# Contiguous query tiles for the row maxima, and the softmax shift turned by TensorE instead of by a DMA

## The reference, cut to what matters

```
q = (xn @ Wq.T + bq) * 16**-0.5;  k = xn @ Wk.T + bk;  v = xn @ Wv.T + bv   # per head: 2048 x 16
scores = einsum('bqhd,bkhd->bhqk', q, k)
probs  = softmax(scores, axis=-1)
out    = einsum('bhqk,bkhd->bqhd', probs, v) @ Wo.T + bo
x + out + ffn(xn)
```

## Time and profile before

| what | value |
|---|---|
| median of 3 runs | 3491.28 us (3490.54 to 3492.51) |
| the profiled execution, its own time | 3490.54 us |
| its span, first to last instruction | 3488.5 us |
| TensorE busy | 3355.6 us, 96% |
| VectorE busy | 2889.4 us, 83% |
| ScalarE busy | 2453.4 us, 70% |
| TensorE weight loads busy | 1892.9 us, 54% |
| mean granted TensorE clock | 0.977 |

### The profile page before, as it was taken

The page is one execution under the profiler, slowest core; times in us unless marked ns, Lnnn a source line. Parts: engine busy times, 40 slices in busy tenths (PEclk is TensorE's granted clock), DMA queues, the critical chain, the costliest instruction groups (busy, mean ns, idle before and its releaser), DMA issues. The chain is left out here.

```text
span 3488.5 us, 69413 instructions
## 1 busy us (share of the span) xinstructions
PE 3355.6 (96%) x19824; PEld 1892.9 (54%) x19824; DVE 2889.4 (83%) x2923; ACT 2453.4 (70%) x4702; POOL 927.9 (27%) x1339
## 2 busy tenths in 40 slices
PE   7869999999999999999999999999999999599998
PEld 6434555555555555555555555555555554288887
DVE  7508999899899999998999999999999997367777
ACT  3552888888788788878888888788788877534333
POOL 2550222222222222222222222222222222144443
PEclk9986999999999999999999999999999999899999
DMA  6670112111112111111221122111111221345553
GB/s 197 181 231 28 50 53 59 56 57 55 55 55 55 54 53 53 53 53 56 57 55 55 54 59 57 55 54 54 53 52 53 57 57 39 110 137 162 159 169 115
DMA packets 142713, 271.57 MB, mean 78 GB/s; under 512 B 32240, under 2 KB 78384, under 8 KB 130160
## 3 DMA queue, kind: packets, MB, share of 16 engines
q1 hardware_dynamic: 140192, 266.68, 26.5%
q10 hardware_dynamic: 2256, 1.36, 0.1%
HBM read 173.59 MB, written 84.93 MB: 74 GB/s over the span
## 5 line engine op out<-in xcount | busy, mean ns | idle before, releaser
L832 DVE TENSOR_REDUCE half_max<-m_ps 128x1 f32<-128x1024 f32 x2048 | 2414.4, 1220 | 377.4 <-PE m_ps L759 372.5
L713 ACT ACTIVATE prob<-s_ps 128x512 f32<-128x512 f32 x4096 | 2122.2, 603 | 547.2 <-PE s_ps L770 542.6
L759 PE MATMUL m_ps<-k_feat,q_feat 48*128 48x512 f32 x4096 | 1576.3, 500 | 39.0 <-DMA k_feat<-k_parts 27.8
L770 PE MATMUL s_ps<-q_feat,k_feat 50*128 50x512 f32 x4096 | 1497.0, 444 | 13.1 <-ACT prob L713 8.1
L759 PEld LDWEIGHTS m_ps<-k_feat,q_feat 48*128 48x128 f32 x4096 | 1052.8, 302 | 233.1 <-DVE half_max L832 197.6
L770 PEld LDWEIGHTS s_ps<-q_feat,k_feat 50*128 50x128 f32 x4096 | 679.3, 184 | 903.9 <-ACT prob L713 875.8
L779 PE MATMUL a_ps<-prob,v_head 128*32 128x512 f32 x8192 | 1094.4, 606 | 0.0
L567 POOL TENSOR_TENSOR shift<-row_max,shift 128x16 fp32r<-128x16 f32 x64 | 14.2, 221 | 1307.0 <-ACT shift L720 1307.0
L779 PEld LDWEIGHTS a_ps<-prob,v_head 128*32 128x32 f32 x8192 | 161.3, 108 | 249.9 <-issue 225.9
L1113 ACT ACTIVATE g_hi<-g 128x512 fp32r<-128x512 f32 x128 | 81.0, 632 | 247.7 <-DVE g L1151 204.7
L1276 POOL TENSOR_TENSOR g_lo<-g,g_hi 128x512 fp32r<-128x512 f32 x128 | 173.0, 1351 | 231.3 <-ACT g_hi L1113 231.3
(11 more groups left out here) (131 smaller groups left out, 1891.7 us busy)
## 6 DMA issues: line engine op xcount, KB each, us to landing
q_feat<-q_parts SPq DMA_DIRECT2D x128, 256.0 KB
k_feat<-k_parts SPq DMA_DIRECT2D x128, 256.0 KB
q_parts<-parts SPq DMA_DIRECT2D x32, 512.0 KB, 4.7
k_parts<-parts SPq DMA_DIRECT2D x32, 512.0 KB, 4.8
q_feat<-q_parts SPq DMA_DIRECT2D x128, 128.0 KB
k_feat<-k_parts SPq DMA_DIRECT2D x128, 128.0 KB
att_dram<-att SPq DMA_DIRECT2D x64, 256.0 KB, 14.2
mask_bc<-mask_b SPq DMA_DIRECT2D x128, 128.0 KB, 4.3
```

Source lines behind the costliest of these rows:

```text
L713: act.activation(prob[tile(r, kt) % R][:, qb * BLK:(qb + 1) * BLK], s_ps[slot(r, kt, qb) % R][:, :], ACT.Exp).then_inc(exped, 1)
L759: ins = pe.matmul(m_ps[p % 2][:, k * BLK:(k + 1) * BLK], q_feat[r % 2][LOW, :].rearrange("c (p q) -> c p q", q=ST)[:, :, qt], k_feat[r % 2 ...
L770: pe.matmul(s_ps[slot(r, kt, qb) % R][:, :], k_feat[r % 2][UP, kt * P:(kt + 1) * P], q_feat[r % 2][UP, qb * BLK:(qb + 1) * BLK], start=Tru ...
L832: dve.tensor_reduce(half_max[r][:, p // 2, p % 2:p % 2 + 1], m_ps[p % 2][:, :], AX.X, ALU.max).then_inc(maxed, 1)
```

## The change

The queries of a tile of the first pass are now neighbours (qt*128 to qt*128 + 127). Row p of `row_max` therefore holds queries 128 apart, and the shift has to be transposed before it can be written as two rows. TensorE does that (`turn`): a transpose of 128 x 32 into the `s_ps` buffer that comes next in the ring, after score 1 of kt = 13. ScalarE copies the 32 x 128 result to the new `shift_t` (`read_shift`) and one DMA writes it. A head therefore has 65 slots in the ring of three, not 64. `round_shift` stays after exponential 2 of kt = 12, and its wait for the last shift DMA moves to `read_shift`. `collect` moves from behind exponential 1 of kt = 1 to behind exponential 3. VectorE's loop has a body of three heads and 20 iterations, not six and 10. `turn` for head 0 stands in the stretch before the first score, ahead of piece 5 of head 1.

```diff
-    ROUND_AT = 12
+    TURN_AT, TURN_AFTER = 13, 1
-    SLOTS = ST * QB
+    SLOTS = ST * QB + 1
+    shift_t = sb("shift_t", [SHIFT * ST, P], F32R)
...
-            def put_shift(n, u):
-                sp.wait_ge(shift_done, n + 1)
-                for k in range(SHIFT):
-                    row = slice(UPPER + FEAT + k, UPPER + FEAT + k + 1)
-                    sp.dma_start(q_feat[u][row, :].bitcast(F32).rearrange("k (p q) -> k p q", q=ST),
-                                 shift[:, k, :].bitcast(F32)).then_inc(shift_in, 16)
+            def put_shift(c, u):
+                sp.wait_ge(exped, c + 1 + R)
+                sp.dma_start(q_feat[u][SHIFT_ROWS, :].bitcast(F32).rearrange("k (q p) -> k q p", p=P),
+                             shift_t[:, :].bitcast(F32)).then_inc(shift_in, 16)
...
+            def read_shift(n, c, u, first=False):
+                act.wait_ge(scored, c + 1)
+                if not first:
+                    act.wait_ge(shift_in, n * 16)
+                act.activation(shift_t[:, :], s_ps[u][0:SHIFT * ST, 0:P], ACT.Copy).then_inc(exped, 1)
...
-                        exp(g, r, kt, qb)
-                        if following and (kt, qb) == (ROUND_AT, QB - 2):
+                        exp(g, r, kt, qb, following)
+                        if following and (kt, qb) == (TURN_AT - 1, QB - 2):
                             round_shift(g + 1, r + 1)
-                        if not first and (kt, qb) == (LAG - 1, 1):
-                            collect(g - 1)
+                        if following and (kt, qb) == (TURN_AT, TURN_AFTER):
+                            read_shift(g + 1, turn_slot(g), turn_slot(r) % R)
+                    if kt == LAG - 1 and not first:
+                        collect(g - 1)
...
-                                q_feat[r % 2][LOW, :].rearrange("c (p q) -> c p q", q=ST)[:, :, qt],
+                ins = pe.matmul(m_ps[p % 2][:, k * BLK:(k + 1) * BLK], q_feat[r % 2][LOW, qt * P:(qt + 1) * P],
...
+            def turn(n, c, u):
+                pe.wait_ge(exped, c + 1)
+                wait_apart(pe, shift_done, n + 1, t["passed"][1])
+                pe.transpose(s_ps[u][0:SHIFT * ST, 0:P], shift[:, :, :].rearrange("p k q -> p (k q)").bitcast(F32),
+                             t["ident"][:, :]).then_inc(scored, 1)
...
-                    score(g, it, r, kt, 1)
+                    score(g, it, r, kt, 1, following)
+                    if following and kt == TURN_AT:
+                        turn(g + 1, turn_slot(g), turn_slot(r) % R)
...
             for p in range(EARLY):
+                if p == EARLY // 2:
+                    turn(0, 0, 0)
...
-            with nc.Fori(0, ROUNDS, engines=[ENGINE.DVE], hint_back_edge=True) as i:
-                for k in range(U):
-                    maxima(i * U + R + k, k % R)
+            with nc.Fori(1, HEADS // R, engines=[ENGINE.DVE], hint_back_edge=True) as i:
+                for r in range(R):
+                    maxima(i * R + r, r)
```

More of the change, by code:

```diff
@@ L492, in attend @@
     EARLY = 10
-    ROUND_AT = 12
+    TURN_AT, TURN_AFTER = 13, 1
     LAG = 2
-    SLOTS = ST * QB
+    SLOTS = ST * QB + 1
     LOADS = 4
     ROUNDS = (HEADS - 4) // U
-    SHIFT_LOADS = SHIFT
     q_feat = [sb(f"q_feat{r}", [P, S], F32R) for r in range(2)]
@@ L543, in attend, with slot, turn_slot @@
     ones_set, ones_made = sem("a_ones_set"), sem("a_ones_made")
-    def slot(g, kt, qb):
-        return g * SLOTS + kt * QB + qb
+    def slot(g, kt, qb, turn=True):
+        return 1 + g * SLOTS + kt * QB + qb + (turn and (kt, qb) > (TURN_AT, TURN_AFTER))
+    def turn_slot(g):
+        return 1 + g * SLOTS + TURN_AT * QB + TURN_AFTER + 1
     def tile(g, kt):
@@ L678, in step @@
                 if following:
-                    put_shift(g + 1, (r + 1) % 2)
+                    put_shift(turn_slot(g), (r + 1) % 2)
                 if third:
@@ L707, in _, with exp @@
                 act.activation(k_feat[u][96:P, :], prob[0][96:P, :], ACT.Copy).then_inc(ones_made, 1)
-            def exp(g, r, kt, qb):
+            def exp(g, r, kt, qb, turn):
                 if qb == 0:
                     act.wait_ge(weighed, tile(g, kt) + 1)
-                act.wait_ge(scored, slot(g, kt, qb) + 1)
-                act.activation(prob[tile(r, kt) % R][:, qb * BLK:(qb + 1) * BLK], s_ps[slot(r, kt, qb) % R][:, :],
+                act.wait_ge(scored, slot(g, kt, qb, turn) + 1)
+                act.activation(prob[tile(r, kt) % R][:, qb * BLK:(qb + 1) * BLK], s_ps[slot(r, kt, qb, turn) % R][:, :],
                                ACT.Exp).then_inc(exped, 1)
             def round_shift(n, r):
-                if not (isinstance(n, int) and n == 0):
-                    act.wait_ge(shift_in, n * 16 * SHIFT_LOADS)
                 act.wait_ge(row_maxed, n + 1)
                 act.activation(shift[:, 0, :], row_max[r % R][:, :], ACT.Copy).then_inc(shift_rounded, 1)
+            def read_shift(n, c, u, first=False):
[3 more added lines that the diff above has]
+                act.activation(shift_t[:, :], s_ps[u][0:SHIFT * ST, 0:P], ACT.Copy).then_inc(exped, 1)
             def collect(g):
@@ L725, in collect, with step @@
                 act.activation(att[:, :], a_ps[:, :], ACT.Copy).then_inc(att_read, 1)
-            def step(g, r, first=False, following=True):
+            def step(g, it, r, first=False, following=True):
                 for kt in range(ST):
                     for qb in range(QB):
-                        exp(g, r, kt, qb)
-                        if following and (kt, qb) == (ROUND_AT, QB - 2):
+                        exp(g, r, kt, qb, following)
+                        if following and (kt, qb) == (TURN_AT - 1, QB - 2):
                             round_shift(g + 1, r + 1)
-                        if not first and (kt, qb) == (LAG - 1, 1):
-                            collect(g - 1)
+                        if following and (kt, qb) == (TURN_AT, TURN_AFTER):
+                            read_shift(g + 1, turn_slot(g), turn_slot(r) % R)
+                    if kt == LAG - 1 and not first:
+                        collect(g - 1)
             round_shift(0, 0)
-            step(0, 0, first=True)
+            read_shift(0, 0, 0, first=True)
+            step(0, 0, 0, first=True)
             with nc.Fori(0, ROUNDS, engines=[ENGINE.Activation], hint_back_edge=True) as i:
                 for r in range(1, U + 1):
-                    step(i * U + r, r)
+                    step(i * U + r, i, r)
             for g in range(1 + ROUNDS * U, HEADS):
-                step(g, g, following=g + 1 < HEADS)
+                step(g, 0, g, following=g + 1 < HEADS)
             collect(HEADS - 1)
@@ L758, in pass1 @@
                 key = half * 2 * BLK + k * BLK
-                ins = pe.matmul(m_ps[p % 2][:, k * BLK:(k + 1) * BLK],
-                                q_feat[r % 2][LOW, :].rearrange("c (p q) -> c p q", q=ST)[:, :, qt],
+                ins = pe.matmul(m_ps[p % 2][:, k * BLK:(k + 1) * BLK], q_feat[r % 2][LOW, qt * P:(qt + 1) * P],
                                 k_feat[r % 2][LOW, key:key + BLK], start=True, stop=True)
@@ L763, in pass1, with score, weigh @@
                     ins.then_inc(piece, 1)
-            def score(g, it, r, kt, qb):
+            def turn(n, c, u):
[3 more added lines that the diff above has]
+                             t["ident"][:, :]).then_inc(scored, 1)
+            def score(g, it, r, kt, qb, turn):
                 if (kt, qb) == (0, 0):
                     wait_fed(r, it, fed_up)
-                    pe.wait_ge(shift_in, (g + 1) * 16 * SHIFT_LOADS)
-                pe.wait_ge(exped, slot(g, kt, qb) + 1)
-                pe.matmul(s_ps[slot(r, kt, qb) % R][:, :], k_feat[r % 2][UP, kt * P:(kt + 1) * P],
+                    pe.wait_ge(shift_in, (g + 1) * 16)
+                pe.wait_ge(exped, slot(g, kt, qb, turn) + 1)
+                pe.matmul(s_ps[slot(r, kt, qb, turn) % R][:, :], k_feat[r % 2][UP, kt * P:(kt + 1) * P],
                           q_feat[r % 2][UP, qb * BLK:(qb + 1) * BLK], start=True, stop=True).then_inc(scored, 1)
-            def weigh(g, r, kt):
+            def weigh(g, r, kt, turn):
                 if kt == 0:
@@ L776, in weigh @@
                     pe.wait_ge(att_read, g + 1)
-                pe.wait_ge(exped, slot(g, kt, QB - 1) + 1 + R)
+                pe.wait_ge(exped, slot(g, kt, QB - 1, turn) + 1 + R)
                 for qb in range(QB):
@@ L794, in step @@
                     a, b = half(kt, 0), half(kt, 1)
-                    score(g, it, r, kt, 0)
+                    score(g, it, r, kt, 0, following)
                     a(0)
                     a(1)
-                    score(g, it, r, kt, 1)
+                    score(g, it, r, kt, 1, following)
+                    if following and kt == TURN_AT:
+                        turn(g + 1, turn_slot(g), turn_slot(r) % R)
                     if kt >= LAG:
-                        weigh(g, r, kt - LAG)
```

(9 more changed lines are left out.)

## The result

| | before | changed |
|---|---|---|
| median | 3491.51 us (4 runs, 3490.54 to 3492.51) | 3545.55 us (4 runs, 3544.39 to 3565.2) |
| ratio, 95% interval | 1 | 1.0168 [1.0133, 1.0203] |
| profiled execution, its own time | 3490.54 us | 3545.07 us |
| its span | 3488.5 us | 3543.3 us |

The changed kernel is 54 us slower, 1.7%. One of its four timed runs took 3565.2 us at a mean granted clock of 0.969 instead of 0.977; it makes the interval as wide as it is.

What follows compares the result with a forecast made beforehand. The prediction took a ring of score 2, exponential, score 1 and weighing, 2.60 us per key tile, to bound the kernel. Its sum was 3490.5 - 6.5 + 33 + 30 - 2 = 3545 us, range 3508 to 3590.

Steps and rivals of the forecast that it cites:

- The bound: What sets the pace of an ordinary key tile: a ring of dependent steps, 2.60 us, before and after.
- Ring: In each key tile: score 2, its exponential, score 1, weighing, next score 2; 2.59 us, no row-maximum matmul in it.
- The turn: Transpose between score 1 and weighing of kt = 13: 0.17 wait plus 0.35 itself per head, +33 us (19 to 40).
- collect: Its later place delays a head's first weighing, at kt = 2, by 0.48 us: +30 us (28 to 35).
- The contiguous load and the loop: End of row maxima: the 0.17 us delay vanishes, 20 loop jumps cost 0.42 each; -6.5 us (-15 to +4.6).
- +4.6 for loads as slow as before: Upper bound at the end of row maxima: loads no faster, 10 new VectorE loop jumps at 0.46 us each.
- The shift's DMA: Issued later, behind `read_shift`, yet landing some 3 us before the next head's first score: no cost.
- Before the first score: Stretch ahead of head 0's scores, with faster loads and head 0's turn: -2 us (-5 to +2).
- faster loads start that copy up to 1.8 us earlier: Before the first score: the lower copy for head 2, ahead of the first shift's DMA, starts up to 1.8 us earlier.
- Loads as the pace: Rival: weight loads limit every key tile, which could shrink to VectorE's 2.36 us, giving 3315 us; chance 0.05.
- One stall hidden: Rival: one of the turn and `collect` stalls, mostly the turn, costs nothing, giving 3512 to 3522 us; chance 0.15.
- A late shift: Rival: TensorE waits 1 to 3 us for the shift at each head's first score, giving 3610 to 3735 us; chance 0.08.

Runs made afterwards that it cites:

- e2: Kernel before with only the contiguous load in the first pass (exponential's argument also scaled by 0.01): 3480.85 us, ratio 0.9967.
- e6: Changed kernel with the strided load of the first pass put back (exponential's argument also scaled by 0.01): 3556.19 us, ratio to before 1.0196.
- e1: Kernel before with only `collect` moved late, behind exponential 3 of kt = 1: 3525.56 us, ratio 1.0104.
- e3: Changed kernel with `collect` moved back early, behind exponential 1 of kt = 1: 3515.83 us, ratio to before 1.0061.
- e4: Changed kernel with VectorE's loop back at a body of six heads: 3543.26 us, ratio to before 1.0144.
- e8: Kernel before with the short reduction of a head's maxima one piece later, behind piece 0 of the next head: 3475.99 us, ratio 0.9952.
- e5: Changed kernel with the turn behind weighing of kt = 13 instead of ahead of it: 3527.14 us, ratio to before 1.0112.
- e7: Changed kernel with `collect` early, VectorE's loop of six and the turn behind weighing: 3492.18 us, ratio to before 1.0001.
- e9: Kernel before with exponentials and v in BF16, so weighing is one pass of matmuls, not two: 3658.16 us, ratio 1.0476.
- e12: Kernel before with BF16 exponentials and v, and each weighing made twice into the same sums: 4058.22 us, ratio 1.1621.

## Why the prediction was right, point by point

- **The bound.** Ring, not loads: 2.60 us before, after, in e2 and in e6. Right.
- **The turn**, +33 us (0.52 per head). Measured 0.46, 63 x 0.46 = 29. The wait was 0.23 and not 0.17 (0.10 from the end of the exponential to the turn's load, where I had 0.05), the turn to weighing 0.23 and not 0.35.
- **collect**, +30 us (0.48 per head over today's place). Measured 0.57 and 0.10 before, so 0.47, and the next distance is 0.03 longer: 0.50, 63 x 0.50 = 31.5. e1 and e3 give 33 and 30.
- **The contiguous load and the loop**, -6.5 us. Measured 19 x 0.40 and 0.15 once, where the loop is entered, 7.8 in all, against 15.1: -7. The loads did get faster, so the +4.6 for loads as slow as before falls. e2 shows the load alone at -12, e4 the loop at +2 (+4 by its trace), against +4 expected.
- **The shift's DMA**, nothing. No wait at a head's first score. Right.
- **Before the first score**, -2 us. Measured nothing that can be told from the scatter: the first score starts at 314.10 and not 314.25, and from the first load of the first pass to it are 57.3 us against 58.3 before, 57.4 in e1 and 56.9 in e8, which have the same loads as before. The step that failed is "faster loads start that copy up to 1.8 us earlier": the copy starts 40.4 us behind the first load, 40.5 before. The shift's DMA goes out at 304.33 and not 298.74, behind the turn, and the first score is no later for it. At the lower clock, which holds in that stretch, VectorE's pairs still start 2.53 apart with a wait of 0.17, as the earlier trace rows have 0.18:

```profile
265.65 2.36 DVE L849 TENSOR_REDUCE half_max<-m_ps 128x1 f32<-128x1024 f32 x2 [0.17 <-PE m_ps L767]
268.18 2.36 DVE L849 TENSOR_REDUCE half_max<-m_ps 128x1 f32<-128x1024 f32 x2 [0.17 <-PE m_ps L767]
```

- **Sum.** 3545 forecast, 3545.07 profiled. The terms as measured: 29 + 31.5 - 7 = 53.5, and head 61 is 1.2 us longer beyond them. Why head 61 is longer is told at e5: the lower clock lasted 13.7 us there and not 6.8. That the total is so near is partly luck: the errors of -4, +1.5, -0.5 and +2 and the 1.2 cancel.
- **The rivals.** Loads as the pace: e2. One stall hidden: e1 and e3. A late shift: no such wait. In e8 a forecast of mine was off by 6 us: I took a jump of VectorE's loop to cost 0.46 whatever stands ahead of it, and without the short reduction there it cost nothing.

## What to carry to other kernels

Before a faster instruction is bought, write down the ring that repeats and ask whether the instruction stands in it; a stretch of the same kernel that lacks the instruction, like this kernel's last head, answers it for nothing. An instruction put into a hand-written order costs what it waits for besides its own time, so put it where its data have long been there: the same turn cost 0.46 behind a score and 0.22 behind the weighing. When an engine is late once per round but not short of time, move its odd job into its own idle time: that gave 16 us here, and the way to the same slack by a contiguous load and a turn gave nothing net, even repaired (e7).

## What the runs showed of the hardware that I had not expected

- The granted clock did not follow TensorE's busy time. With BF16 weighing TensorE was busy 989 us of 1000 at a clock of 0.50, with every weighing doubled 1000 of 1000 at 0.50, and with 32-bit floats 997 of 1000 at 1.00. In all three the clock stood at 0.50 from some 230 us on, before the first score; the 32-bit kernel went up again at 327 us, the two others only behind `attend` (e9 at 3212 us). With the cheaper operand type everything beside weighing ran at the lower clock too: a score's matmul took 0.71 in the mean of e12, 0.44 before. It is not the number of matmuls, which e12 has in common with the kernel before; what in the BF16 weighing keeps the clock down is open.
- A strided load of 128 columns took 0.29 at either level of the clock. A contiguous one took 0.18 at 2.4 GHz and 0.28 to 0.29 at 1.2 (the scores' loads of e9). So the stride costs 0.11 at the full clock and nothing at the lower one, which is why the contiguous load did not speed up the stretch before the first score. The Trainium skill, "SBUF — State Buffer", section "Specifications (TRN2)", speaks of 16-byte lines and a penalty for each access that crosses to a new one; a stride of 64 bytes crosses at each element. The loads at the full clock agree, 302 ns against 188; those at the lower clock show no penalty.
- The gap at the jump of VectorE's loop, 0.46 in the earlier trace rows right behind the short reduction, is gone in e8, where another reduction of a piece stands ahead of the jump, though the next piece is there already.
- TensorE's loop jumps left no excess at a clock of 1.00, and up to 3.3 us each in e9, at 0.50.
